# In the main loop of a transformer block on TensorE, two up-projection chunks in a row and then two eighths of the down-projection, instead of one and one

## The reference

```python
x = x + attn(layernorm(x), wq, wk, wv, wo)
x = x + ffn(layernorm(x), W_fc, W_proj)

# attn: linear attention without softmax
energy = einsum('bnd,bne->bde', K, V); context = einsum('bnd,bde->bne', Q, energy) * sqrt(3/64)
out = einsum('bnd,ed->bne', context, wo)

# ffn: 256 -> 1024 -> 256, and five steps of a spiking neuron on the result
h = square(relu(einsum('bsd,fd->bsf', x, W_fc)));  y = einsum('bsf,df->bsd', h, W_proj)
mem = 0.9 * mem + y - (mem > 1) * 1;  spike = mem > 1        # 5 times
return sum(spikes) / 5
```

## Time and profile before

| | us |
|---|---|
| median of 3 runs | 469.25 (469.23 to 472.36) |
| the profiled execution | 474.71, its span 472.9 |
| TensorE (PE) busy | 458.9 |
| VectorE (DVE) busy | 367.0 |
| ScalarE (ACT) busy | 281.7 |
| GpSimd (POOL) busy | 238.3 |

### The profile page before, as it was taken

One profiled execution on the slowest core, in us unless ns is written; L12 is line 12 of the kernel. 1 busy time (PEld: TensorE's weight loads), 2 busy tenths in 40 slices (PEclk: granted clock), 3 DMA queues, 4 the chain that ended last, 5 costly groups with the idle time before them and its releaser, 6 DMA issues. The chain is left out here.

```text
span 472.9 us, 8194 instructions
## 1 busy us (share of the span) xinstructions
PE 458.9 (97%) x2844; PEld 403.7 (85%) x2844; DVE 367.0 (78%) x922; ACT 281.7 (60%) x521; POOL 238.3 (50%) x196
## 2 busy tenths in 40 slices
PE   8999999999999999999999999999999999999993
PEld 7577898988989888898889889898898989898993
DVE  4768677878788787879868788886879886767657
ACT  3559756665566666556576655757565565656530
POOL 2019465655556554655655555565545653444430
PEclk9999999999999999999999999999999999999998
DMA  8614034341524434252353425244241404040111
GB/s 275 159 45 91 0 51 128 91 125 55 134 46 98 125 79 128 64 134 44 90 134 83 125 62 134 46 120 104 66 90 39 122 1 111 24 115 21 44 46 44
DMA packets 120969, 41.29 MB, mean 87 GB/s; under 512 B 114016, under 2 KB 114656, under 8 KB 120672
## 3 DMA queue, kind: packets, MB, share of 16 engines
q1 hardware_dynamic: 120928, 40.78, 33.9%
HBM read 25.03 MB, written 15.73 MB: 86 GB/s over the span
## 5 line engine op out<-in xcount | busy, mean ns | idle before, releaser
L398 POOL TENSOR_TENSOR hid_l<-hid,hid_h 128x512 fp32r<-128x512 f32 x128 | 167.2, 1309 | 187.6 <-ACT hid_h L453 187.6
L443 ACT ACTIVATE relu<-hid_ps 128x512 f32<-128x512 f32 x128 | 76.2, 596 | 117.9 <-PE hid_ps L894 117.0
L892 PE MATMUL y_ps<-wdn_h,hid_h 128*128 128x256 f32 x480 | 136.2, 284 | 0.0
L893 PE MATMUL y_ps<-wdn_l,hid_h 128*128 128x256 f32 x480 | 135.7, 283 | 0.0
L894 PE MATMUL y_ps<-wdn_h,hid_l 128*128 128x256 f32 x480 | 135.7, 283 | 0.0
L892 PE MATMUL hid_ps<-x2T_h,wup_h 128*128 128x512 f32 x256 | 105.6, 412 | 0.8 <-DVE x2T_l L706 0.8
L893 PE MATMUL hid_ps<-x2T_l,wup_h 128*128 128x512 f32 x256 | 100.8, 394 | 0.0
L894 PE MATMUL hid_ps<-x2T_h,wup_l 128*128 128x512 f32 x256 | 100.0, 391 | 0.0
L892 PEld LDWEIGHTS y_ps<-wdn_h,hid_h 128*128 128x128 f32 x480 | 91.5, 191 | 9.7 <-POOL hid_l L398 5.1
L775 DVE SCALAR_TENSOR_TENSOR cnt<-y_ps,bound,cnt 128x256 f32<-128x256 f32 x240 | 98.5, 472 | 0.2
L893 PEld LDWEIGHTS y_ps<-wdn_l,hid_h 128*128 128x128 f32 x480 | 91.6, 191 | 4.2
(11 more groups left out here) (151 smaller groups left out, 571.3 us busy)
## 6 DMA issues: line engine op xcount, KB each, us to landing
xs<-x_dram SPq DMA_DIRECT2D x15, 512.0 KB, 4.7
out_dram<-x SPq DMA_DIRECT2D x15, 512.0 KB, 2.6
x_blocks<-x SPq DMA_DIRECT2D x56, 128.0 KB, 2.7
x_block<-x_blocks SPq DMA_DIRECT2D x14, 512.0 KB, 3.7
x_block<-x_dram SPq DMA_DIRECT2D x104, 64.0 KB, 2.6
hid<-w_up_dram SPq DMA_DIRECT2D x1, 1024.0 KB, 8.3
x<-w_down_dram SPq DMA_DIRECT2D x1, 1024.0 KB, 10.4
xs<-x_dram SPq DMA_DIRECT2D x2, 256.0 KB, 3.6
```

The costliest lines, as they stand in the source:

```text
L398: nc.gpsimd.tensor_tensor(hid_l[:, i % 2, c, :], hid[:, c % 4, :], hid_h[:, i % 2, c, :].bitcast(f32), ALU.subtract).then_inc(hid_ready, 1)
L443: nc.scalar.activation(relu[:, c % 2, :], hid_ps[c % 2][:, :], ACT.Relu).then_inc(relu_done, 1)
L892: mm(dst, a[0], b[0], start=start, stop=False)
L893: mm(dst, a[0], b[1], start=False, stop=False)
```

## The change

In step 1 to 15, an even c emits chunks c and c + 1 one behind the other, and an odd c emits no chunk. The eighths and the other work keep their c.

```diff
                 for c in range(FC):
-                    if there(r, i):
+                    if there(r, i) and c % 2 == 0:
                         project_up(r, i, c)
+                        project_up(r, i, c + 1)
                     if there(r, i - 1):
                         project_down(r, i - 1, c)
                     if c == 0 and there(r, i + 2):
                         project_q(r, i + 2)
                         energy_sum(r, i + 2)
```

## The result

The changed kernel takes 474.62 us (median of 8 runs, 474.23 to 475.21), the kernel before 471.21 us in the runs beside it (8 runs, 469.23 to 472.36). The ratio is 1.0083, with an interval of 1.0064 to 1.0102: slower by 0.8%, about 3.9 us (the medians differ by 3.4). The spread is part of the result: the eight runs of the changed kernel lie within 1.0 us, those of the kernel before within 3.1, and its profiled execution, on which the prediction was built, took 474.71.

What follows compares the result with a forecast made beforehand. TensorE, 97% busy, was taken as the bound, with only waits to save: stalls -2.8 us and round trip +4.3 gave +1.5 on the profiled 474.71; less the 5.5 us difference to the median, 470.7 us, range 466.0 to 475.5.

Steps and rivals of the forecast that it cites:

- D0's stall goes: TensorE's wait between U0 and D0 vanishes as U1 fills it: -0.24 us in seven even steps and step 15, -1.9.
- EO, odd steps: Q starts 1.15 us later, but VectorE is busy until 220.93, so energy and EO come only 0.2 us later.
- ATT's stall goes: ATT, now wanted 1.39 us later behind U3, loses its 0.42 us wait for eo_l in five odd steps.
- The pair's second chunk, KV, TURN: U(c+1)'s rectified input and kvT's copy arrive in time: no wait, at most some 0.3 us a step.
- The round trip: x1's scatter and gather start 1.39 us later against the next U0, making steps 1, 4, 7, 13, 14 late: +4.3 us.
- The fetch as cause of the long scatters: A 16 KB instruction packet during the scatter lengthens residual to gather, 6.7 against 4.8 us, in steps 1, 4 and 7.
- the second rival: Long scatters vanish, as fetches don't cause or no longer meet them: 467.8 us, or 466.4; chance 0.20.
- I carry the difference over unchanged.: The runs' median, 469.25, lies 5.5 us below the profiled execution, 474.71; the same difference was applied to the forecast.

Runs made afterwards that it cites:

- second profile of before: The kernel before, unchanged, profiled and timed again against itself: ratio 0.9992, median 470.29 us, profile span 468.2 us.
- cheap race: POOL's low half of kv (L377) cut to 8 of 64 columns: in the kernel before 469.63 us (0.9980), in the changed kernel 474.45 us (1.0081).

## Why the prediction came out as it did

Forecast: 470.7 us as a median of 469.25 plus 1.5, within 1%; measured: 474.62 us, +0.8%, inside the range, but +3.4 to +3.9 us where the sum said +1.5. Of the 3.9 us by which 474.62 lies above the forecast, 2.0 are its base: the median of 3 runs was 469.25, that of 8 is 471.21. Against the execution on which it was made, the sum gave +1.5 and the profile after gives +0.5. That this looks close, and that the change stayed within 1%, is in part luck: the sum was made on an execution that had lost its races. By its steps:

- **D0's stall goes.** Right for the even steps to 12, which are 0.27 to 0.29 us shorter (0.24 expected), and the wait named after hid_l is gone. But steps 14 and 15, which the sum took in, had no such stall: there D0 started 0.23 us after the last matmul of U0 before the change too, so 0.5 us of the -1.9 was not there. That y_free was the releaser is what the code says. The runs don't tell it from hid_l: in step 7 before, L398 and the fourth L775 both end 1.5 us after U0, and D0 now starts 2.9 us after it, behind either.
- **EO, odd steps: "of 1.15 us only 0.2 us reaches it".** This is the step that failed. The sum took the time at which VectorE came to q, 5.89 us after U0, for a property of the kernel. It was the outcome of a race lost in every odd step from 3 to 13 of that one execution. Where VectorE wins, it waits for q already, and q's delay is passed on in full: from 4.91 to 6.04 us after U0 (222.10 - 216.06), 1.13 us. In the changed kernel q is later than VectorE even after a lost race (by 0.18 us at 222.10, though the two L778 there took 1.85), so it always pays what the kernel before paid only when it lost. Against a won step an odd step is 28.09 - 27.46 = +0.63 us where the sum had -0.22. Against a lost one it is -0.31, near the sum, and this is why the two profiles agree so well.
- **ATT's stall goes.** Right against the lost steps; but in the won ones there was none (ATT at 224.31 follows D2's last at 224.19 in the second profile of before), so nothing was to be had.
- **The pair's second chunk, KV, TURN: nothing.** Right; TURN doesn't wait in steps 1 to 15, and the pairs from U4 on left the step lengths alone.
- **The round trip, +4.3 us.** Right in mechanism, and near in size: U0 waits in steps 1, 4, 13 and 14, 3.6 us in all; from the second profile of before to the one after, these four steps grow by 1.41, 0.61, 1.14 and 0.63 us, which holds the EO and D0 terms too. Step 7 was not late: its scatter met the fetch at its very start and its handover was 5.0 us. Step 1 was late by 1.5 instead of 0.83, since its handover took 6.85 us instead of 6.5 and its gather 4.0 instead of 3.7. The deviations cancel in part: 3.6 us for the 4.3 of the sum. That no other step got late is right as well.
- **The fetch as cause of the long scatters.** Shown by moving it. The rule that the Trainium skill (Runtime: NRT & Kernel Launch, section Instruction fetch mechanics) gives, that crossing a block is mostly hidden, fits TensorE's pace (matmuls 0.23 us apart at 231 us in the first profile of before) and not the scatter of small packets beside it; the second rival's way out (fetches that meet no scatter) can't be had by a shift alone, since they meet others.
- **"I carry the difference over unchanged."** The 5.5 us between profile and median were not overhead. The profiled execution of the changed kernel is only 0.6 us above its median. The size of that difference was the warning that the profile showed an execution at the slow end of the spread.

The full account against an execution without lost races, from the second profile of before to the one after: odd steps 3 to 11, 5 x 0.64 = +3.2 us; even steps 2, 6, 8, 10, 12, 5 x -0.29 = -1.4; steps 1, 4, 13 and 14, +3.8; in all +5.5 us (5.1 between the spans, as U0 of step 1 comes 0.4 us earlier after). With a cheap race in both it is 4.8; there the profile of the changed kernel has steps 1 and 4 at 29.07 and 27.41 us instead of 29.45 and 27.64, so the length of the late round trips changes from execution to execution too. The medians of the kernel before, 470.2 to 471.8 in four batches, lie 0.6 to 2.1 us above its version with the cheap race; what it loses there the changed kernel doesn't lose again. Beside the result it was 471.21, 1.6 above, which leaves 3.2 of the 4.8 us; measured were 3.4 to 3.9.

## What to carry to other kernels

Before a chain of waits is priced from one profiled execution, compare that execution's time with the runs: where it lies at the edge of their spread, look for instructions of one group with two lengths (here 0.42 and 1.52 us), and work the sum out for both. When work is moved ahead of a producer, follow the producer's delay to the consumer that already waits, and put the consumer, not the producer, behind the moved work: the same pairs were 0.8% slower with EO ahead of U2 and 0.4% faster with EO behind it. And a step that shortens the way between a transfer's start and its use can be taken only where that way has room; chosen step by step, and with EO behind U2 or Q ahead of U1, the change became a gain of 0.9%, of which 0.6% remain against the kernel before with its race made cheap.

## What the runs showed of the hardware

- Two VectorE instructions with two SBUF inputs each in a row (L778), and a GpSimd one (L377) that starts 0.05 us behind the first: either the second VectorE instruction is held (1.52 us instead of 0.42) or the GpSimd one (1.87 instead of 1.51), and which one changes from step to step and from execution to execution. The kernel before ran in 468.9 to 474.7 us; with the GpSimd instruction cut short, 12 runs lay within 1.1 us.
- Such a wait counts as busy time: VectorE's busy time was 367.0, 358.6 and 347.5 us in three profiles with the same instructions (before, before again, after). From the first to the second the race (L778, 33.6 to 25.1 us) accounts for it; from the second to the third it is L666 (14.0 to 3.9) and L670 (5.2 to 3.0), which no longer meet L398.
- One 16 KB fetch of instructions during a scatter of 0.52 MB in 4160 packets lengthens the handover by some 1.7 to 2.0 us (4.85 to 6.5 and 6.85); at the scatter's very start (step 7 after) it costs 0.1 us.
- Blocks of 512-column and 256-column matmuls in turn cost nothing over two blocks of each: even steps take 27.03 to 27.05 us with the pairs from U4 on, and 27.03 to 27.05 without.
